# Odd slots of layer 0 and every slot of layer 1: value products moved ahead of scores on TensorE

## What is computed

```python
x = x + _L0_attn_ref(_layernorm(x), ...)     # causal linear attention, 16 heads of 16, features elu + 1
x = x + _L0_xattn_ref(_layernorm(x), ctx_1024, ...)   # softmax attention, 16 heads, over 77 context rows
x = x + _L0_ffn_ref(_layernorm(x), ...)      # 16 experts, top 2, capacity 640
x = x + _L1_attn_ref(_layernorm(x), ...)     # 8 heads of 64 over a latent of 64, softmax over 256 keys
x = x + _L1_xattn_ref(_layernorm(x), ctx_1024, ...)   # one head over 77 context rows
x = x + _L1_ffn_ref(_layernorm(x), ...)      # gated, quantised, inner width 768
```

```python
scores = q @ latent.T ; attn = softmax(scores) ; out = attn @ latent   # then one projection for all heads
```

## Time and profile before

| What | Value |
|---|---|
| Median of 3 runs | 1672.96 us (1669.79 to 1673.18) |
| The profiled execution | 1675.36 us, its span 1673.6 us |
| Mean granted clock of TensorE | 0.968 of full |
| TensorE busy over the span | 1536.0 us, 92% |
| VectorE, ScalarE, GpSimd busy | 979.0, 842.2, 468.4 us |
| Layer 1's attention stage | about 931 to 1340 us |

### The profile page before, as it was taken

How to read it: one execution, slowest core, us unless ns; L and a number is a source line. 1 busy time by engine, 2 the same in 40 slices (tenths; PEclk the granted TensorE clock), 3 DMA queues, 4 the chain that set the end, 5 groups by cost and what they waited for, 6 DMA issues and landing times. The chain is left out here.

```text
span 1673.6 us, 27432 instructions
## 1 busy us (share of the span) xinstructions
PE 1536.0 (92%) x10279; PEld 1083.3 (65%) x10279; DVE 979.0 (58%) x2296; ACT 842.2 (50%) x1849; POOL 468.4 (28%) x592
## 2 busy tenths in 40 slices
PE   8999999998987899999999899999999989996299
PEld 5676767766755777787777466666666654442288
DVE  3665766767766435222222567766664568777883
ACT  4446555555555422211212565666656533597980
POOL 4223234253234410000002665555542300032100
PEclk9999999999998999999999999999999889998599
DMA  3440111011151154334424211110100000000031
GB/s 115 156 156 18 47 30 44 30 47 44 34 165 39 61 164 137 125 113 126 153 87 136 70 39 52 43 34 27 39 14 14 1 25 1 0 1 15 24 99 65
DMA packets 100929, 108.32 MB, mean 65 GB/s; under 512 B 25410, under 2 KB 89804, under 8 KB 100800
## 3 DMA queue, kind: packets, MB, share of 16 engines
q1 hardware_dynamic: 94656, 90.01, 17.3%
q0 software_dynamic: 6144, 16.57, 3.1%
HBM read 64.77 MB, written 42.01 MB: 64 GB/s over the span
## 5 line engine op out<-in xcount | busy, mean ns | idle before, releaser
L1795 POOL TENSOR_SCALAR c_pr<-c_pr,c_rsum 128x256 f32<-128x256 f32 x256 | 128.2, 518 | 190.2 <-DVE c_rsum L2211 189.8
L2089 ACT ACTIVATE c_pr<-bank,c_nmax 128x256 f32<-128x256 f32 x256 | 118.0, 473 | 119.9 <-DVE c_nmax L2206 119.8
L1526 ACT ACTIVATE b_G<-bank 128x320 f32<-128x320 f32 x128 | 56.0, 437 | 210.8 <-PE bank L1475 210.8
L1475 PE MATMUL bank<-b_XT,shared 128*128 128x320 f32 x512 | 154.6, 437 | 0.0
L2206 DVE TENSOR_REDUCE c_nmax<-bank 128x2 f32<-128x512 f32 x128 | 82.4, 685 | 108.6 <-PE bank L1854 108.5
L1489 PE MATMUL bank<-shared,b_G 128*128 128x256 f32 x640 | 142.2, 379 | 0.0
L1489 PEld LDWEIGHTS bank<-shared,b_G 128*128 128x128 f32 x640 | 120.9, 190 | 17.8
L1072 DVE TENSOR_TENSOR hT_all<-bank,a_causal 128x512 f32<-128x512 f32 x128 | 79.4, 682 | 67.5 <-PE bank L563 67.5
L498 POOL TENSOR_TENSOR a_L<-a_L,a_Lm 128x1232 f32<-128x1232 f32 x32 | 72.0, 2249 | 149.5 <-DVE a_Lm L1087 149.5
L1475 PEld LDWEIGHTS bank<-b_XT,shared 128*128 128x128 f32 x512 | 92.5, 193 | 27.6 <-issue 1.2
L1545 DVE COPY b_Y<-bank 128x256 f32<-128x256 f32 x80 | 33.9, 424 | 120.3 <-PE bank L1489 120.1
(11 more groups left out here) (376 smaller groups left out, 3400.2 us busy)
## 6 DMA issues: line engine op xcount, KB each, us to landing
shared<-L_ffn_w SPq DMA_DIRECT2D x32, 512.0 KB, 6.0
t_slots_in<-a_h SPq DMA_DIRECT2D x20, 512.0 KB, 7.5
shared<-t_slots_in SPq DMA_DIRECT2D x15, 640.0 KB, 7.3
t_slots_out<-b_Y SPq DMA_DIRECT2D x15, 640.0 KB, 4.1
hT_all<-x SPq DMA_DIRECT2D x8, 512.0 KB, 4.0
a_xr<-x SPq DMA_DIRECT2D x8, 512.0 KB, 3.9
t_x_a<-a_x SPq DMA_DIRECT2D x8, 512.0 KB, 2.9
shared<-t_x_a SPq DMA_DIRECT2D x8, 512.0 KB, 4.3
```

The costliest lines, as they stand in the source:

```text
L1475: t = p.matmul(P[2 + n % 2][:, 0:HC], w1[e % 3][:, u, 128 * f:128 * f + 128], XT[e % 2][:, u, HC * m:HC * m + HC], start=(u == 0), stop=(u ...
L1795: p.tensor_scalar(pr[k][:, e, u, :], pr[k][:, e, u, :], rsum[k][:, e, u:u + 1], 1.0, ALU.mult, ALU.mult).then_inc(q.pr_ready, 1)
L2089: a.activation(pr[t % 2][:, e, u, :], P[e][:, S * u:S * u + S], ACT.Exp, bias=nmax[t % 2][:, e, u:u + 1], accum_out=sums[t % 2][:, e, u:u ...
```

## The change

In layer 1 `values(t - 2)` is issued ahead of `scores(t)` instead of behind `turn(t - 1)`, and on ScalarE `heads(t - 2)` goes ahead of `exponents(t)`. In layer 0 `values` of an odd slot goes ahead of `x_scores`; `x_values` of the second batch moves from slot 2 into slot 3, that of the first batch from slot 6 into slot 7, both between the two. ScalarE's copies of them move along, `turn_norm(2, ...)` goes ahead of `to_tokens` in slot 3, and the table of banks follows.

```diff
-                 2: (("proj1", -1), ("xproj0", -3), ("xval1a", -3), ("xval1b", -3), ("pkt", 1)),
+                 2: (("proj1", -1), ("xproj0", -3), ("pkt", 1)),
...
-                 7: (("val3", 0),) + tuple((n, -2) for n in turned(2)) + (("xq0", -1),)}
+                 7: (("val3", 0), ("xval0a", -2), ("xval0b", -2)) + tuple((n, -2) for n in turned(2)) + (("xq0", -1),)}
...
                     if s % 2 == 0 and now:
                         scores(g, s // 2)
+                    if s % 2 and now:
+                        values(g, s // 2)
+                    if s == 3 and back3:
+                        x_values(g - 3, 1)
+                    if s == 7 and back2:
+                        x_values(g - 2, 0)
                     if s % 2 and back2:
                         x_scores(g - 2, s // 2)
-                    if s % 2 and now:
-                        values(g, s // 2)
...
                     if s == 3:
                         if back2:
                             x_turn(g - 2, 0)
+                        if back4:
+                            turn_norm(2, g - 4, h2[(g - 4) % 2])
                         if back3:
...
                             to_tokens("xtok3", g - 3, oxT, 3)
-                        if back4:
-                            turn_norm(2, g - 4, h2[(g - 4) % 2])
...
                     if s == 7:
                         if back2:
+                            keep_x_values(g - 2, 0)
                             by_key(g - 2, 2)
...
                     late, behind, ahead = there(g - 2), there(g - 1), there(g + 1)
+                    if t >= 2:
+                        values(t - 2)
                     scores(t)
...
                     if t >= 1:
                         turn(t - 1)
-                    if t >= 2:
-                        values(t - 2)
...
                     late, behind, ahead = there(g - 2), there(g - 1), there(g + 1)
+                    if t >= 2:
+                        heads(t - 2)
                     exponents(t)
...
-                    if t >= 2:
-                        heads(t - 2)
```

More of the change, by code:

```diff
@@ L303, in layer0 @@
                  1: (("val0", 0),) + tuple((n, -3) for n in turned(3)) + (("col1", -1), ("xcol0", -3), ("xk", -1), ("v0", 1)),
-                 2: (("proj1", -1), ("xproj0", -3), ("xval1a", -3), ("xval1b", -3), ("pkt", 1)),
-                 3: (("val1", 0),) + tuple((n, -2) for n in turned(0)) + (("xtok2", -3), ("xtok3", -3), ("turn2a", -4), ("turn2b", -4), ("xv", -1)),
+                 2: (("proj1", -1), ("xproj0", -3), ("pkt", 1)),
+                 3: (("val1", 0), ("xval1a", -3), ("xval1b", -3)) + tuple((n, -2) for n in turned(0)) + (("turn2a", -4), ("turn2b", -4), ("xtok2", -3), ("xtok3", -3), ("xv", -1)),
                  4: (("tok0", 0), ("tok1", 0), ("q0", 1), ("q1", 1), ("xcol1", -3), ("logits", -4)),
                  5: (("val2", 0),) + tuple((n, -2) for n in turned(1)) + (("col0", 0), ("xproj1", -3), ("v1", 1), ("gate", -4)),
-                 6: (("proj0", 0), ("turn1a", -1), ("turn1b", -1), ("xval0a", -2), ("xval0b", -2), ("turn0a", 2), ("turn0b", 2),
+                 6: (("proj0", 0), ("turn1a", -1), ("turn1b", -1), ("turn0a", 2), ("turn0b", 2),
                      ("rank", -4), ("state0", 1), ("state1", 1)),
-                 7: (("val3", 0),) + tuple((n, -2) for n in turned(2)) + (("xq0", -1),)}
+                 7: (("val3", 0), ("xval0a", -2), ("xval0b", -2)) + tuple((n, -2) for n in turned(2)) + (("xq0", -1),)}
         place, used, front, turn_of = {}, [0, 0, 0, 0], {}, 0
@@ L810, in _ @@
                             project("xproj0", g - 3, axT, xwo, 0)
-                            x_values(g - 3, 1)
                         if ahead1:
@@ L860, in _ @@
                             turn_norm(1, g - 1, h1)
-                        if back2:
-                            x_values(g - 2, 0)
                         if ahead2:
@@ L992, in _ @@
                     if s == 2:
-                        if back3:
-                            keep_x_values(g - 3, 1)
                         if ahead1:
@@ L999, in _ @@
                     if s == 3:
+                        if back3:
+                            keep_x_values(g - 3, 1)
                         if back2:
@@ L1027, in _ @@
                             keep_norm(1, g - 1, hT1)
-                        if back2:
-                            keep_x_values(g - 2, 0)
                         if ahead2:
@@ L2027, in _ @@
                         project(g, 0)
+                values(TAIL - 2)
                 scores(TAIL)
                 turn(TAIL - 1)
-                values(TAIL - 2)
                 project(Z, 0)
```

## The result

| | before | after |
|---|---|---|
| Median of the runs | 1673.07 us (1669.79 to 1675.62, 6 runs) | 1713.49 us (1709.65 to 1714.95, 6 runs) |
| The profiled execution | 1675.36 us | 1709.65 us |
| Mean granted clock of it | 0.968 | 0.961 |

The ratio is 1.0242, 95% interval 1.0226 to 1.0258: 40 us by the medians, where 24 were forecast. The profiled execution of after is the fastest of its six, so the two traces lie only 34 us apart.

What follows compares the result with a forecast made beforehand. TensorE, busy 94% of the second layer, was taken to end nearly every slot. Profiled 1675.36 us, +25 second layer, -3.5 first layer, +3 clock, gave 1699.9, median 1697; forecast 1684 to 1709 (chance 0.62), range 1673 to 1717.

Steps and rivals of the forecast that it cites:

- Direction and main cause: Second layer: values (L1880) wait for ScalarE's copy of the probabilities (L2102), some 30 us; slower given 0.81.
- step 1: Steady group, second layer: values wait for the copy of P, slot 4.12 to 6.43 us, +2.31.
- Price of a change of tiling: TensorE pays about 0.17 us per change between matmul groups; column to row counted as one full change.
- Steps 7 and 0: Steady group, second layer: TensorE's filler covers all, so each gains the saved change, -0.17 us.
- The eight steps: Slots of a steady second-layer group: +2.66 us a group together, +13.3 over five groups.
- Step 6: Steady group, second layer: context scores need the turned stream, then values follow; 7.10 to 7.86 us, +0.76.
- Groups 0 and 1: First second-layer groups, with shorter fillers: 85.96 us for 15 slots becomes 96.6, less 1.0 of values moved out, +9.7.
- The last group: End of second layer: gains back long POOL waits, pays at its two 3.1 us slots, +2 us.
- The clock: TensorE's falls from 2.4 to 1.2 GHz in stretches with waits: two falls of 1.7 us counted, +3.
- The rival with a fall in every group: Clock falls in every group, or first layer adds a wait per group: 1709 to 1722 us, chance 0.16.
- Layer 0: First layer: -3.5 us; ends -20 (all changes and waits gone) and +8 (one more wait per group).
- the gain forecast for layer 0's full groups: First layer, six groups with a full pipeline: net -0.55 us a group.

Runs made afterwards that it cites:

- filled waits: Layer 1 as changed, layer 0 as before, useless transposes on TensorE while it waits for the transposed probabilities; 1712.21 us against before's 1687.42, ratio 1.0152.
- the one group in five above: Steady group in layer 1 with values three slots behind, ahead of scores in every step, layer 0 as before: 53.8 us instead of 52.2; kernel 1.0009 against before.
- the two halves of layer 0's change: Against before, layer 1 unchanged: only the values ahead of the context scores, ratio 1.0053; only the context value products moved, ratio 1.0105.
- the two runs: Layer 0 as changed with layer 1 of before, run twice: 1677.72 us against before's 1670.91, and 1679.25 against 1672.61.
- the kernel 2.0% slower: Layer 1 as changed with layer 0 of before: 1705.67 us against before's 1670.91, ratio 1.0200.
- the same kernel on the two: Layer 1 values three steps behind, ahead of scores only in steps 2, 3 and 7, layer 0 as before: 1678.70 us against before's 1687.42, and 1660.88 against 1672.61.

## Why the prediction was right, and where it was not

- **Direction and main cause: right and shown.** The forecast named L1880 idle behind L2102 with some 30 us: 30.8. Taking the wait away by a slot more of lag takes the loss away (1.0009). In step 1 only 1.23 of the forecast 2.3 us stand at L1880; another 0.93 stand at L1890 behind VectorE, a wait that the forecast did not have and that ends inside the same step.
- **Price of a change of tiling: right.** Values step at 1.01, scores at 1.07, and column to row costs like any other. Steps 7 and 0, where nothing waits, moved by -0.19 and +0.16; the second was to lose 0.17, but its context value products now stand 0.2 us for a copy.
- **The eight steps: right.** Forecast +2.31, -1.49, +1.27, -0.35, +0.50, +0.76, -0.17, -0.17, together +2.66 a group; measured +2.30, -1.51, +1.05, -0.38, +0.48, +0.74, -0.19, +0.16, together +2.65. That the sum agrees to 0.01 is luck, since steps 3 and 0 err against each other. Step 6 has a slip as well: its terms 4.83, 1.91 and 1.02 add up to 7.76 and not 7.86; with the 0.07 for the release that the other steps have it is 7.83, and 7.84 was measured.
- **Groups 0 and 1: right without the clock.** Forecast +9.7; with filled waits +9.4, as run +12.6.
- **The last group: mis-sized.** Forecast +2; as run +7.8 in after. Filled, 45.0 us, it is +2.1 over before's 42.9, but before's contains a fall of its own: the two halves of layer 0's change, which have before's layer 1, had none there and took 40.7. So the order costs 4.3 in this group and the clock 6.
- **The clock: the term that failed.** The forecast took +3, two falls for the whole kernel. Layer 1 lost 9 us to it, layer 0's seventh group some 3 more. The error was to count two falls of 1.7 us from the earlier trace rows: the first two groups had two new ones, and the last group, where waiting slots follow each other with thin fillers, 17 us at half rate. The rival with a fall in every group was wrong too: the five steady groups of after show none, and they take 54.4 us filled or not. The passage of the Trainium skill from which the prediction took 14 us (TensorE: Matmul & The Clock Gate, "HAM oscillation") tells of a kernel that loses the clock in every round because it waits some 3 to 5 us for a DMA after about 2 us of matmuls. The longest wait of a steady group here is 1.23 us, so the prediction carried the passage further than it goes, and no run here tests it. That short waits keep the clock safe does not follow: see the one group in five above.
- **Layer 0: wrong sign.** Forecast -3.5, range -20 to +8 (six groups at -0.55 are -3.3); the medians of the two runs are 6.8 and 6.6 us above their before. Two steps failed. Each moved block was followed to ScalarE and to the banks, and not through VectorE's list: the context scores behind the values feed VectorE, whose division comes late, and TensorE waits for it (0.65 to 2.06 us a group). And the groups behind the full pipeline had no term at all, though the moved products were the cover of the rank sums there.
- **The sum.** Layer 1 +25 against 33.6 (24.6 without the clock), layer 0 -3.5 against +6: 24 forecast, 40 measured. Of the miss of 16 us, some 6 are falls of the clock at the ends of layer 1 and 4 are the seventh group of layer 0 (3 of them again the clock), which a steady group does not show; the rest is the gain forecast for layer 0's full groups, which did not come. That layer 1 without the clock comes so near to its forecast (24.6 and 25) is partly luck: before's own fall in the last group, some 2 us, hides as much of the order's price.

## What to carry to other kernels

Before a group of matmuls is moved ahead of others to save a change of tiling (0.17 us here), ask what it was covering: the work that comes next behind its old place will wait for its inputs in the open, and where an input is made only one slot before, another slot of lag took the wait away here, and another order of the copies did not. Move it only in the steps where neither holds, and the change, with a slot more of lag, is worth 0.4 to 0.6% here instead of costing 2.4. Cost the first groups, the last group and the tail by themselves: less work stands there to cover a wait, and the clock falls on top of it.

## What the runs showed of the hardware

- After 2.95 us of waiting TensorE went on at 1.2 GHz, for 6.8 us in all, while the five steady groups of after, with waits of up to 1.23 us and 5.6 us of waiting in 54, stayed at 2.4 GHz.
- Two groups with the same matmuls and the same waits can differ in the clock: of five steady groups with three slots of lag, none with a wait over 1.35 us, four kept 2.4 GHz and one had 3.4 us at 1.2 GHz, for 1.6 us more.
- Dummy transposes of 0.13 us each in the waits kept the clock at 1.00 in the last group (0.83 without), and delayed nothing in the steady groups (54.4 us with and without): worth 9 us of 426.
- The mean clock of a whole run says little of where time is lost: the kernel 2.0% slower ran at 0.961 to 0.967, the one it is compared with at 0.966 to 0.973.
- The same kernel took 1671 us on one chip and 1687 on another, and there one group of unchanged code took 43.9 us instead of 38.3. The cause is open; ratios to runs on the same chip held (0.9957 and 0.9939 for the same kernel on the two).
